# Three main products moved behind the gates of a two-layer mixture kernel, and results kept where they are

## The reference, cut to what matters

```
x = x + ffn0(cond0(x))                       # 8 experts, top 2 of 8 per row
c = conv1d(x, weight, taps 9, groups 4) + (cond @ c_weight.T)[:, :, None] + bias
h = relu(layernorm(c @ gw1.T + gb1)); gates = h @ gw2.T + gb2
top_v, top_i = top_k(gates, 2); top_g = softmax(top_v)
allowed = (onehot(top_i).sum over all rows <= capacity)      # needs every row's gate
w = onehot * top_g * allowed
lora = sum over experts of ((c @ lora_A) * w) @ lora_B / 16
x = x + c @ weight.T + lora
```

## Time and profile before

| | before |
|---|---|
| median of 3 runs | 852.18 us (850.26 to 853.11) |
| the profiled execution | 853.87 us, its span 852.0 us |
| TensorE busy | 816.2 us, 96% of the span |
| VectorE busy | 399.9 us, 47% |
| chain that ended last | TensorE 81%, DMA 6%, VectorE 6% |

### The profile page before, as it was taken

The page is one execution under the profiler, slowest core; times in us unless marked ns, Lnnn a source line. Parts: engine busy times, 40 slices in busy tenths (PEclk is TensorE's granted clock), DMA queues, the critical chain, the costliest instruction groups (busy, mean ns, idle before and its releaser), DMA issues.

```text
span 852.0 us, 13067 instructions
## 1 busy us (share of the span) xinstructions
PE 816.2 (96%) x4260; PEld 674.0 (79%) x4261; DVE 399.9 (47%) x920; ACT 216.5 (25%) x335; POOL 90.4 (11%) x137
## 2 busy tenths in 40 slices
PE   6999599999999999999999999999999999999985
PEld 5555488888888888888888888888898898889863
DVE  1388650241514215142151151486566566656597
ACT  2344241342514325242252242300100010000100
POOL 1000121011110111011110012121112111100000
PEclk9999699999999999999999999999999999999998
DMA  8888479373555525555255254675545644520048
GB/s 284 347 323 311 176 278 418 114 256 127 185 183 181 201 86 184 184 169 213 86 174 192 90 197 132 214 204 140 126 98 139 147 108 107 155 58 25 1 137 258
DMA packets 61652, 149.26 MB, mean 175 GB/s; under 512 B 6928, under 2 KB 23584, under 8 KB 60704
## 3 DMA queue, kind: packets, MB, share of 16 engines
q1 hardware_dynamic: 40960, 93.41, 33.4%
q0 software_dynamic: 9968, 36.19, 14.6%
q10 hardware_dynamic: 10704, 19.41, 6.0%
HBM read 100.74 MB, written 39.85 MB: 165 GB/s over the span
## 4 chain that ended last, share of the span: by engine, by line
PE 81%; DMA 6%; DVE 6%; issue 3%; ACT 2%; SPq 1%; ACTq 1%; DVEq 0%; POOL 0%; POOLq 0%
PE bank L1283 58%; PE bank L1322 6%; PE bank L1181 4%; PE bank L1331 4%; PE bank L1274 3%; DMA work<-in_expert_w 3%; PE bank L1385 1%; DVE work L1116 1%; PE bank L1158 1%; DVE weights L937 1%; PE bank L1229 1%; PE bank L1204 1%; PE bank L1144 1%; DMA work<-y_scratch,pos_c 1%; DMA x1p<-res 1%
## 5 line engine op out<-in xcount | busy, mean ns | idle before, releaser
L1283 PE MATMUL bank<-weights,l_hi 128*128 128x512 f32 x1696 | 523.8, 390 | 0.0
L1283 PEld LDWEIGHTS bank<-weights,l_hi 128*128 128x128 f32 x1696 | 319.4, 188 | 64.6
L1283 PE MATMUL bank<-weights,l_lo 128*128 128x512 f32 x848 | 336.0, 396 | 2.5 <-DVE l_lo L905 2.4
L1283 PEld LDWEIGHTS bank<-weights,l_lo 128*128 128x128 f32 x848 | 159.7, 188 | 35.5 <-issue 4.5
L905 DVE TENSOR_TENSOR l_lo<-bank,l_hi 128x512 fp32r<-128x512 f32 x37 | 25.6, 692 | 184.0 <-ACT l_hi L684 184.0
L937 DVE TENSOR_TENSOR weights<-work,weights 128x1024 fp32r<-128x1024 f32 x64 | 76.2, 1223 | 55.1 <-ACT weights L695 54.8
L695 ACT ACTIVATE weights<-work 128x1024 fp32r<-128x1024 f32 x64 | 65.1, 1054 | 45.9 <-DMA work<-in_expert_w 27.6
L540 POOL DMA_INDIRECT work<-c_scratch,idx x37 | 42.4, 1146 | 196.2 <-PE bank L1274 195.9
L1322 PE MATMUL bank<-conv_sb,x1p 128*128 128x128 f32 x512 | 59.8, 275 | 1.1 <-DMA x1p<-res 1.1
L1322 PEld LDWEIGHTS bank<-conv_sb,x1p 128*128 128x128 f32 x512 | 58.8, 192 | 1.4 <-DMA x1p<-res 1.3
L735 ACT ACTIVATE l_hi<-work 128x512 fp32r<-128x512 f32 x32 | 18.4, 621 | 158.4 <-PE bank L1283 157.8
(11 more groups left out here) (174 smaller groups left out, 514.5 us busy)
## 6 DMA issues: line engine op xcount, KB each, us to landing
work<-in_expert_w SPq DMA_DIRECT2D x68, 512.0 KB, 6.3
y_scratch<-work ACTq DMA_DIRECT2D x74, 256.0 KB, 2.0
res<-in_x SPq DMA_DIRECT2D x16, 512.0 KB, 14.4
c_scratch<-work SPq DMA_DIRECT2D x16, 512.0 KB, 3.0
out<-work SPq DMA_DIRECT2D x16, 512.0 KB, 4.2
res<-in_x_ph SPq DMA_DIRECT2D x14, 512.0 KB, 5.4
x1p<-res SPq DMA_DIRECT2D x112, 64.0 KB, 4.6
work<-in_x_t SPq DMA_DIRECT2D x6, 1024.0 KB, 6.9
```

Of the source, the lines that this page charges most:

```text
L1283: mm = pe.matmul(to[:, :], a[:, k, :], b[:, k, cols * HALF:(cols + 1) * HALF], start=(k == 0 and n == 0), stop=(k == HC - 1 and n == 2))
```

## The change

- Only main(0) to main(12) stay in the old order. Behind main(12) stand down(13), conv(14), conv(15), down(14), down(15), main(13), the ones product, the first half of main(14), the transposes, the second half of main(14), up products 0 to 10, the first half of main(15) with tile 15's up product in the same accumulation, up products 11 to 14, the second half of main(15) with its up product. conv(15) uses banks 6 and 7.
- c1 has three rows for the last three tiles, and tile 14 has its own l_hi2 and l_lo2.
- VectorE combines tiles 14 and 15 one after the other, before gate(12); its last steps follow TensorE's new order.
- The weights' columns are in natural order. `take_main` reads `res` with the stride and writes the sum in natural order one row lower (`res[t-1]`, tile 0 in `first_out`); `take_up` adds in place with plain access, and SP stores from there. The ring of four rows and its waits are gone. Up products use 3 pairs of banks. Tile 15 has no add for its up product: one add and one store for each half, 256 KB each.
- lora_B's and the transposes' rounded parts lie in buffers of their own, so lora_B is rounded before the main products are done.

```diff
-RING = 4
...
+EARLY_UPS = 11
...
-        ring = [row(j) for j in range(RING)]
-        c1 = row(4).rearrange("p (c m) -> p c m", c=HC)
+        c1_rows = [row(n).rearrange("p (c m) -> p c m", c=HC) for n in (4, 0, 2)]
...
-        lora_sb = row(0)
-
+        lora_sb = row(1)
...
+        def c1_of(t):
+
+            return c1_rows[max(t - (NT - 3), 0)] if isinstance(t, int) else c1_rows[0]
+
+        def parts(t):
+
+            return (l_hi2, l_lo2) if isinstance(t, int) and t == NT - 2 else (l_hi, l_lo)
+
+        def result(t):
+
+            if isinstance(t, int):
+                return res[:, t - 1, :] if t > 0 else first_out[:, :]
+            return res[:, bass.ds(t - 1, 1), :].rearrange("p o n -> p (o n)")
...
+            def store(t, cols):
+                to = out[tile_rows(t), cols].rearrange("(m c) n -> c m n", c=CP)
+                sp.dma_start(to, result(t)[:, cols]).then_inc(s_out, 16)
+
+            for t in range(EARLY_UPS):
+                sp.wait_ge(s_fin, 2 * (t + 1))
+                store(t, slice(0, H))
+            sp.wait_ge(s_me0, NT + CREDIT)
+            store(NT - 1, slice(0, HALF))
+            for t in range(EARLY_UPS, NT - 1):
+                sp.wait_ge(s_fin, 2 * (t + 1))
+                store(t, slice(0, H))
+            sp.wait_ge(s_me1, NT + CREDIT)
+            store(NT - 1, slice(HALF, H))
+            sp.wait_ge(s_out, 16 * (NT + 1))
...
+                if not isinstance(t, int) or t < NT - 2:
+                    act.wait_ge(s_m1, t)
+                elif t == NT - 1:
+                    act.wait_ge(s_m1, NT - 2)
...
+            root(NT - 3)
+            round_c(NT - 2)
+            root(NT - 2)
+            root(NT - 1)
+            act.wait_ge(s_lora, 16)
+            act.wait_ge(s_c1, NT * 2)
+            for h in range(2):
+                act.activation(up_hi[:, h, :], lora_sb[:, h * HALF:(h + 1) * HALF], ACT.Copy).then_inc(s_uh, 1)
             act.wait_ge(s_d2, 1)
             act.activation(we[:, :], wd[:, :], ACT.Exp).then_inc(s_ex2, 1)
-
-            act.wait_ge(s_m0, NT)
-            act.wait_ge(s_lora, 16)
-            for h in range(2):
-                act.activation(up_hi[:, h, :], lora_sb[:, h * HALF:(h + 1) * HALF], ACT.Copy).then_inc(s_uh, 1)
+            round_c(NT - 1)
...
+                at = 6 if isinstance(t, int) and t == NT - 1 else 4
...
-            def take_main(t):
-                rows = res[:, bass.ds(t, 1), :].rearrange("p o n -> p (o n)")
-                for h, (s, done) in enumerate(((s_m0, s_me0), (s_m1, s_me1))):
-                    dve.wait_ge(s, t + 1)
-                    half = rows[:, h * HALF:(h + 1) * HALF]
-                    dve.tensor_tensor(half, bank[h][:, :], half, ALU.add).then_inc(done, 1)
+            def take_main(t, halves=range(2)):
+
+                rows = res[:, bass.ds(t, 1), :].rearrange("p o (q w) -> p (o w) q", q=PH)
+                to = result(t).rearrange("p (w q) -> p w q", q=PH)
+                for h in halves:
+                    w = slice(h * P // 2, (h + 1) * P // 2)
+                    dve.wait_ge((s_m0, s_m1)[h], t + 1)
+                    dve.tensor_tensor(to[:, w, :], bank[h][:, :].rearrange("p (w q) -> p w q", q=PH), rows[:, w, :],
+                                      ALU.add).then_inc((s_me0, s_me1)[h], 1)
 
...
                 assert ch.n == 2 * LC, ch.n
-            ch = Chain(dve, s_chC, (NT // 2 - 1) * 2 * LC)
+            ch = Chain(dve, s_chC, (NT // 2 - 2) * 2 * LC)
+            t = NT - 4
+            rest_c(t)
+            for j in range(2):
+                combine(ch, NT - 2 + j, j, NT // 2 - 1)
+            gate(ch, t)
+            take_conv(t + 1)
+            take_main(t)
+            rest_c(NT - 3)
+            gate(ch, NT - 3)
+            take_conv(NT - 2)
+            take_conv(NT - 1)
+            gate(ch, NT - 2)
+            gate(ch, NT - 1)
             rest_c(NT - 2)
-            gate(ch, NT - 2)
-            take_conv(NT - 1)
-            take_main(NT - 2)
-            rest_c(NT - 1)
-            gate(ch, NT - 1)
-
+            take_main(NT - 3, [0])
...
+            take_main(NT - 3, [1])
             for h in range(2):
...
-            take_main(NT - 1)
+            rest_c(NT - 1)
+            dve.wait_ge(s_me1, NT - 2 + CREDIT)
+            take_main(NT - 2, [0])
 
...
-            with dve.Fori(0, NT // RING) as i:
-                for j in range(RING):
-                    t = i * RING + j
-                    rows = res[:, bass.ds(t, 1), :].rearrange("p o (q w) -> p (o w) q", q=PH)
-                    to = ring[j].rearrange("p (w q) -> p w q", q=PH)
-
-                    dve.wait_ge(s_out[j], i * 16 + DMA_CREDIT)
-                    for h in range(2):
-                        dve.wait_ge(s_up, t * 2 + h + 1)
-                        w = slice(h * P // 2, (h + 1) * P // 2)
-                        dve.tensor_tensor(to[:, w, :], bank[2 * (1 - j % 2) + h][:, :].rearrange("p (w q) -> p w q", q=PH),
-                                          rows[:, w, :], ALU.add).then_inc(s_fin, 1)
+            take_main(NT - 2, [1])
+
+            def take_up(t):
+                for h in range(2):
+                    half = result(t)[:, h * HALF:(h + 1) * HALF]
+                    dve.wait_ge(s_up, t * 2 + h + 1)
+                    dve.tensor_tensor(half, bank[2 + t % 3 * 2 + h][:, :], half, ALU.add).then_inc(s_fin, 1)
+
+            for t in range(EARLY_UPS):
+                take_up(t)
+            take_main(NT - 1, [0])
+            for t in range(EARLY_UPS, NT - 1):
+                take_up(t)
+            take_main(NT - 1, [1])
...
+            def up(t, to, h, start):
+
+                q, at = t // TG, (t % TG) * P
+                for n, (a, b) in enumerate(((twt_lo, up_hi), (twt_hi, up_hi), (twt_hi, up_lo))):
+                    mm = pe.matmul(to[:, :], a[:, q, at:at + P], b[:, h, :], start=(start and n == 0), stop=(n == 2))
+                return mm
+
+            def main(t, halves=range(2), more=False):
+                for h in halves:
+                    pe.wait_ge((s_me0, s_me1)[h], t + CREDIT)
                     for k in range(HC):
                         if h == 0 and k % 4 == 0:
                             pe.wait_ge(s_cl, t * 2 + k // 4 + 1)
-                        mm = product(k, bank[h], w_hi[0], w_lo[0], h)
-                    mm.then_inc(s, 1)
+                        mm = product(k, bank[h], w_hi[0], w_lo[0], h, more, parts(t))
+                    if more:
+                        mm = up(t, bank[h], h, False)
+                    mm.then_inc((s_m0, s_m1)[h], 1)
...
-            with pe.Fori(0, NT // 2 - 1) as i:
+            with pe.Fori(0, NT // 2 - 2) as i:
                 for j in range(2):
                     down(i * 2 + j)
                     conv(1 - j, (i + 1 + j) * (PH * 16), (i * 2 + j + 1) * 2)
                     main(i * 2 + j)
+            down(NT - 4)
+            conv(1, (NT // 2 - 1) * (PH * 16), (NT - 3) * 2)
+            main(NT - 4)
+
+
+
+            down(NT - 3)
+            conv(0, NT // 2 * (PH * 16), (NT - 2) * 2)
+            conv(1, NT // 2 * (PH * 16), None, 6)
             down(NT - 2)
-            conv(1, NT // 2 * (PH * 16), (NT - 1) * 2)
-            main(NT - 2)
             down(NT - 1)
-            main(NT - 1, True)
-
-
+            main(NT - 3)
+            pe.wait_ge(s_a2, NT + CREDIT)
...
+            def ups(tiles):
+
+                for t in tiles:
+                    if t % TG == 0:
+                        pe.wait_ge(s_tl, t // TG + 1)
+                    if t in (1, 2):
+                        pe.wait_ge(s_tl, 2 * t)
+                    if t >= 3:
+
+                        pe.wait_ge(s_fin, (t - 2) * 2)
+                    for h in range(2):
+                        up(t, bank[2 + t % 3 * 2 + h], h, True).then_inc(s_up, 1)
+
             pe.wait_ge(s_ul, 2)
-            for t in range(NT):
-                q, at = t // TG, (t % TG) * P
-                if t % TG == 0:
-                    pe.wait_ge(s_tl, q + 1)
-                if t == 1:
-
-                    pe.wait_ge(s_me1, NT + CREDIT)
-                if t >= 2:
-
-                    pe.wait_ge(s_fin, (t - 1) * 2)
-                for h in range(2):
-                    for n, (a, b) in enumerate(((twt_lo, up_hi), (twt_hi, up_hi), (twt_hi, up_lo))):
-                        mm = pe.matmul(bank[2 * (1 - t % 2) + h][:, :], a[:, q, at:at + P], b[:, h, :], start=(n == 0), stop=(n == 2))
-                    mm.then_inc(s_up, 1)
+            main(NT - 2, [1])
+            ups(range(EARLY_UPS))
+            main(NT - 1, [0], True)
+            ups(range(EARLY_UPS, NT - 1))
+            main(NT - 1, [1], True)
```

87 lines of the change are left out of this document (46 added, 41 removed).

## The result

| | before | changed |
|---|---|---|
| median | 852.64 us (850.26 to 853.82, 4 runs) | 841.75 us (839.61 to 843.96, 4 runs) |
| ratio | | 0.9876, 95% interval 0.9842 to 0.9910 |
| profiled execution, its span | 853.87, 852.0 us | 839.61, 837.9 us |
| from down(13)'s start to the end of the span | 86.08 us | 76.26 us |

The kernel is 10.9 us faster by the medians, 7.7 to 13.5 by the interval. The prediction said 9.8 us and 842.4 us. The last row of the table is the sharper measure, since TensorE's order ahead of down(13) is the old one and its period there is still 16.64 us a tile: 852.0 - 765.92 before, 837.9 - 761.64 after, a gain of 9.82 us. Each kernel has one profiled execution, so how far the stretch repeats in one kernel is not measured; variants whose end should be the same read 76.24 to 76.26 and 79.45 to 79.47 us, though.

What follows compares the result with a forecast made beforehand. VectorE's adds, 1.94 us a tile, were taken to pace the last 31 us. 814.41 + 1.25 + 22.2 = 837.9, plus 4.3: span 842.2, or 842.4 us against the median; own range 840.5 to 844.2, widened to 840.3 to 846.0.

Steps and rivals of the forecast that it cites:

- The reorder's waits: Between main(12) and main(13): TensorE waits 0.5 us for c1, down(15) starts 0.7 us late; together 1.25, bounds 0.5 to 2.5.
- The gates' chain and the transposes: VectorE's gates and weighting, done at 796.0 while TensorE is busy until 797.4: cost nothing, 1.4 us to spare.
- Tile 15's early input: Spread of tile 15 for conv(15), wanted at 771.58: lands at 768.2 to 771.5, so nothing is late.
- rival 3: Tile 15's input is late before conv(15), which waits 7.1 us: 849.5 us; chance 0.04.
- Strided take_main in the loop: Layer 1's loop: 0.7 us a tile more on VectorE, hidden by 4.24 us idle; uncovered 11.2 us.
- Up products: Tail: plain adds of 0.69 us let TensorE's pace of 1.37 us a tile hold, 22.2 us for 16 tiles.
- The end: Behind TensorE's last matmul: one strided add, one 256 KB store landing in 2.6 us, and the close: 4.3 us, before 6.88.
- the stores' limit: Stores in the up products: 285 to 322 GB/s; 15.5 tiles at 1.84 us end at 837.0, close but not the bound.
- 1: Rival for the tail: the stores set the end, deciding below 265 GB/s: 844.2 to 846 us; chance 0.11.
- 2: Rival for the gates: margins of 1.0 to 1.4 us are missed or banks come free late: 843.5 to 846; chance 0.08.
- 4: Rival for the up products: take_up no faster than the old strided add, 1.94 to 2.09 us a tile: 848.5; chance 0.04.
- 5: Rival for layer 1's loop: strided take_main, with gate and combine, makes VectorE the bound, price 11.2 us: 853.6; chance 0.03.

Runs made afterwards that it cites:

- the crossed adds: Changed kernel with the up products' plain adds made in steps of 8 elements, same sums: stretch 81.19 us against 76.26, ratio to before 0.9925.
- the first variant: Changed kernel's adds, three pairs of banks and stores from res, with the orders of the kernel before put back: stretch 79.46 us, ratio to before 0.9924.

## Why the prediction was right

- **What bounds.** VectorE's strided adds set the pace of the old tail: shown, by the cheap adds in the old order (6.6 us gained) and by the crossed adds in the new one (4.9 us lost).
- **The reorder's waits.** Predicted 0.5 us before down(14) for c1 and 0.7 before down(15) for bank 2. The first is not drawn as idle time, and down(14) starts up to 0.46 us late; the second is drawn as 0.57 and is 0.84 with the drain. main(13) starts 14.76 us after down(13) (776.40 - 761.64), predicted 14.8 (780.7 - 765.92). From down(13)'s start to the first up product predicted 38.9 us (804.8 - 765.92), measured 38.71 (800.35 - 761.64).
- **The gates' chain and the transposes** were hidden, as said: no idle time before L1441. The spare time at the comparison was 1.24 us.
- **Tile 15's early input.** Hidden: conv(14) and conv(15) are one row without a gap. SP issued its spread from 757.12 to 762.19, and by the landing times there (2.4 to 3.6 us) some 2 us were to spare before conv(15) at 767.3; the 4 us of margin that rival 3 names were too many, also by the prediction's own 768.2 to 771.5 against 771.58. Its price if late was said to be 7.1 us; it is 8.8, since the clock falls too. That term was too small, in a rival that did not come.
- **Strided take_main in the loop.** Hidden: VectorE still idled 1.21 us before its last in step 12, the step with two combines, and 3.4 to 3.6 us before it in the steps ahead.
- **Up products.** 1.37 us a tile and plain adds of 0.69 us: measured 1.37 and 0.691. TensorE's end 71.98 us after down(13)'s start (837.9 - 765.92), measured 71.87.
- **The end.** 4.3 us predicted, 4.4 measured (837.9 - 833.51), with 2.9 us to landing where I took 2.6. That 9.82 meets 9.8 so closely is partly chance: TensorE's end is 0.1 early and the tail 0.1 long.
- **The range.** Waits of 0.5 to 2.5 and a landing of 2.0 to 4.2 us give 841.1 to 845.2 around 842.4, and not the 840.5 to 844.2 that the forecast states; 841.75 lies in both.
- **What was mis-sized: the stores' limit.** I took DMA share for a gauge and divided (279 / 0.98 and 303 / 0.94), 1.63 to 1.84 us a tile. In the first variant the share stands at 0.92 to 1.02 over rates from 258 to 399 GB/s; its one full queue has a mean of 348 GB/s, 1.5 us a tile, and two queues reach 377. The conclusion held, but the argument gave the reorder no price of its own. With the same adds it is worth 3.2 of the 9.8 us, all through the end of the stores.
- **The rivals.** 1 was the right mechanism for a kernel without main(15) at the end, and is out for this one. 2 did not occur. 4 is out: take_up costs 0.691 us; in the crossed variant adds of 1.165 us cost 4.9 us, where I had said 6. 5 is out, by the idle time above.

## What to carry to other kernels

Give the costly access form to a stage where its engine has idle time, and the cheap one to the stage where that engine sets the pace: the same number of adds, moved, was two thirds of this gain. When compute hands over results faster than stores drain, keep some compute that writes little for the end, so that it covers the queue; splitting the last store or adding a queue did not help here. An early input that feeds a dense stream deserves some microseconds of margin, because a late one costs its wait and then the clock.

## What the runs showed of the hardware that was not expected

- A DMA share near 1 does not tell how near the limit is: 0.92 went with 258 GB/s and 1.01 with 399 GB/s, in the same stage of one trace. The rate over a long full queue tells more, and even that depends on the issue: over the same 16 us 352 GB/s from SP's queue alone, 377 from SP's and ScalarE's.
- SP's issue of a 512 KB store lengthens from 0.56 to 1.19 us in the median (1.67 at most) while the queue is full; with every other store on ScalarE's queue it is 0.56 again and the end is the same, and the landing takes 6.2 to 6.5 instead of 5.8 us.
- An fp32 add of 512 elements with one operand read in steps of 128 elements costs 1.05 to 1.07 us, with all three in steps of 8 elements 1.17 us, plain 0.69 us.
- Behind 6.28 us without work TensorE's granted clock was 0.50, which is the lower of its two levels, 1.2 GHz, from 775 to 779. It rose to 1.00 during the convolution: the mean is 0.64 over 779 to 781.6, and 1.00 from 781.6 on.
